# First chunk of each batch prepared ahead, last batch written out, and some loads and steps issued later

## The reference

```python
mod = (_silu(L0_c) @ L0_wmod).reshape(L0_c.shape[0], 6, 1, -1)
sa, ca, ga, sb, cb, gb = (mod[:, 0], mod[:, 1], mod[:, 2], mod[:, 3], mod[:, 4], mod[:, 5])
...
h = _layernorm(x, axis=-1) * (1 + ca) + sa
x = x + ga * _L0_attn_ref(h, L0_attn_Wqkv, L0_attn_bqkv, L0_attn_Wo, L0_attn_bo)
h = _layernorm(x, axis=-1) * (1 + cb) + sb
x = x + gb * _L0_ffn_ref(h, L0_ffn_gate_weight, L0_ffn_gate_up_proj, L0_ffn_down_proj, L0_ffn_old_to_new)
return x
```

## Time and profile before

| | |
|---|---|
| median of 3 runs | 4376.86 us (4376.18 to 4387.05) |
| profiled execution | 4383.56 us, of which the span of its instructions 4381.8 us |
| mean granted TensorE clock | 0.939 |
| busy share of the span | PE 88%, DVE 62%, POOL 63%, ACT 41% |
| first batch, from first to next first projection | 107.3 to 1053.2 us |
| experts, first to last PE work | from 3913.3 us |

### The profile page before, as it was taken

How to read it: one execution, slowest core, us unless ns; L and a number is a source line. 1 busy time by engine, 2 the same in 40 slices (tenths; PEclk the granted TensorE clock), 3 DMA queues, 4 the chain that set the end, 5 groups by cost and what they waited for, 6 DMA issues and landing times.

```text
span 4381.8 us, 85215 instructions
## 1 busy us (share of the span) xinstructions
PE 3863.3 (88%) x21344; PEld 2343.0 (53%) x21344; DVE 2732.0 (62%) x5837; ACT 1803.8 (41%) x3526; POOL 2773.6 (63%) x2251
## 2 busy tenths in 40 slices
PE   2989999886989998877899998869899998859998
PEld 1755544455744554456654454447555444547776
DVE  2767677455757766465667775457676774546555
ACT  1335555422345555333355554323355554211111
POOL 2768788723768878615678888407587886315454
PEclk7989999997989999988899999979899998979999
DMA  5443333243433334234433333324433332449998
GB/s 193 160 136 81 97 97 105 79 146 105 172 111 95 81 98 122 69 142 134 162 89 95 98 97 103 135 83 160 140 79 97 96 104 79 146 124 257 259 249 194
DMA packets 305622, 555.81 MB, mean 127 GB/s; under 512 B 59892, under 2 KB 99956, under 8 KB 301812
## 3 DMA queue, kind: packets, MB, share of 16 engines
q1 hardware_dynamic: 283640, 491.91, 37.6%
q0 software_dynamic: 21504, 58.40, 5.7%
HBM read 318.15 MB, written 174.85 MB: 113 GB/s over the span
## 4 chain that ended last, share of the span: by engine, by line
PE 60%; issue 14%; POOL 11%; DMA 6%; DVE 4%; ACT 2%; SPq 2%; DVEq 0%; POOLq 0%; ACTq 0%
PE PS L1293 16%; PE PS L1269 12%; PE PS L1246 12%; PE PS L1190 5%; PE PS L1390 4%; POOL qs L951 3%; POOL t L948 3%; PE PS L1401 2%; DMA out<-z,it 2%; POOL Sm L974 2%; DMA QK<-qkd 2%; POOL hTl L926 2%; PE PS L1327 2%; PE PS L1272 1%; SPq L681 1%
## 5 line engine op out<-in xcount | busy, mean ns | idle before, releaser
L1091 ACT ACTIVATE Pt<-PS 128x512 f32<-128x512 f32 (+3 forms) x2560 | 1204.3, 543 | 1069.7 <-PE PS L1269 613.0
L974 POOL TENSOR_TENSOR Sm<-Pt 128x512 f32<-128x512 f32 (+3 forms) x960 | 1028.3, 1077 | 451.7 <-ACT Pt L1091 448.9
L1570 DVE TENSOR_REDUCE part<-PS 128x1 f32<-128x512 f32 x1536 | 1003.7, 685 | 350.1 <-PE PS L1246 342.9
L1246 PE MATMUL PS<-QK 96*128 96x512 f32 (+3 forms) x2560 | 1033.6, 422 | 125.1 <-DMA QK<-qkd 51.1
L1269 PE MATMUL PS<-QK 97*128 97x512 f32 (+3 forms) x2560 | 996.7, 410 | 42.3 <-DMA QK<-mT 21.0
L1293 PE MATMUL PS<-Pt,V 128*32 128x512 f32 (+3 forms) x5120 | 873.5, 555 | 19.4 <-POOL Sm L974 19.3
L1297 PE MATMUL PS<-Sm,onesv 128*32 128x512 f32 (+3 forms) x1920 | 822.0, 536 | 0.0
L1566 DVE CUSTOM_DVE_ANT_0 PS<-PS,consts 128x128 f32<-128x128 f32 (+3 forms) x1024 | 504.0, 495 | 454.8 <-PE PS L1246 449.3
L1269 PEld LDWEIGHTS PS<-QK 97*128 97x128 f32 x2560 | 491.1, 194 | 477.8 <-issue 349.8
L974 POOL TENSOR_TENSOR Sm<-Sm,Pt 128x512 f32<-128x512 f32 (+1 forms) x640 | 712.2, 1113 | 50.2
L1246 PEld LDWEIGHTS PS<-QK 96*128 96x128 f32 x2560 | 501.5, 197 | 333.8 <-DVE part L1570 107.2
(11 more groups left out here) (164 smaller groups left out, 4821.9 us busy)
## 6 DMA issues: line engine op xcount, KB each, us to landing
QK<-qkd SPq DMA_DIRECT2D x720, 128.0 KB, 3.1
qkd<-st SPq DMA_DIRECT2D x64, 1024.0 KB, 4.5
Wg<-wgu SPq DMA_DIRECT2D x48, 768.0 KB, 5.6
o<-od SPq DMA_DIRECT2D x448, 64.0 KB, 2.0
W<-wd SPq DMA_DIRECT2D x4, 6144.0 KB, 21.6
Wd<-wdn SPq DMA_DIRECT2D x48, 384.0 KB, 7.2
xin<-x SPq DMA_DIRECT2D x16, 1024.0 KB, 7.6
vd<-vst SPq DMA_DIRECT2D x16, 1024.0 KB, 6.1
```

Of the source, the lines that this page charges most:

```text
L974: nc.gpsimd.tensor_tensor(total, of[0][:, first:CH] if i == 1 else total, of[i][:, first:CH], ALU.add).then_inc(sum_done, 1)
L1091: nc.scalar.activation(Pt[:, t % NPT, first:CH], S2[t % NS2][:, first:CH], ACT.Exp, scale=SCALE).then_inc(exp_done, 1)
L1246: mm(s1[:, 0:w], QK[0:3 * HD, hh % 2, 0, qb * P:(qb + 1) * P], QK[0:3 * HD, hh % 2, 1, c * CH:c * CH + w], start=True, stop=True).then_inc ...
L1570: v.reduce_max(part[:, qb, cc:cc + 1], s1[:, 0:w], AX.X).then_inc(s1_dve, 1)
```

## The change

Chunk 0 of a batch is no longer prepared by `front()`. For batch 0 its `stat`, `xhat`, turns, `upper` and `lower` stand in the setup, ahead of the loop; for batches 1 to 3 they stand in the third stage of the batch before, as the steps `lead_stat` (behind `old`, ahead of `new` of chunk 3), `lead_xhat` (behind `new`, ahead of `place`) and `lead` (ahead of the last `slot`). They use banks 0 and 1 of PSUM. The scales and shifts modb are copied in two halves. x and the rotary tables of the next batch are loaded behind W's reload; those of batch 0 near the start. SP's wait for the store of W is gone from the setup; ACT waits for it ahead of the first exponential. `batches` makes a loop of three passes and the fourth batch as code of its own behind it, with the number of the batch a constant; there the reload of W and the lead steps are left out. `load_attention` and `load_tokens` for j = 0 and 1 move from the end of hh = 14 into hh = 15, behind its stack, its row of maxima and `move(14, 0)`. The two `widen` steps go from rounds 211 and 217 to rounds 224 and 230. OUT_AT changes.

```diff
-    out = [("stat", 0), ("xhat", 0)]
-    for ct in range(KT):
-        out += parts(0, ct)
+    out = []
...
-OUT_AT = (8, 9, 10, 11, 12, 13, 14, 16)
+OUT_AT = (10, 10, 11, 12, 13, 14, 15, 16)
...
-    closing[NR * (H - 2) + 1].append(("widen", 0))
-    closing[NR * (H - 2) + 7].append(("widen", 1))
+    closing[last - 1].append(("widen", 0))
+    closing[last + 5].append(("widen", 1))
...
+        out += [("back", j, t) for t in range(TPC)] + [("old", j, 0), ("old", j, 1)]
+        if j == NCH - 1:
+            out.append(("lead_stat", j))
+        out.append(("new", j))
+        if j == NCH - 1:
+            out.append(("lead_xhat", j))
...
-    return out + [("slot", NCH - 1)]
+    return out + [("lead", NCH - 1), ("slot", NCH - 1)]
...
+        def batches(eng):
+
+            with eng.Fori(0, NB - 1) as b:
+                yield b
+            yield NB - 1
...
+            def load_lead(b):
+
+                sp.dma_start(xin[0][:, :, :], x[b, 0].rearrange("(t p) c -> p t c", p=P)).then_inc(x_in[0], 16)
+                load_tables(0)
+                load_tables(1)
+
+            load_lead(0)
             wait_apart(sp, mod_done, 1)
...
             sp.dma_start(wd, W[:, :, :, :, :].bitcast(F32)).then_inc(w_out, 16)
-            wait_apart(sp, w_out, 16)
...
-                load_input(0)
-                load_tables(0)
-                load_tables(1)
                 meet(sp, 2 * b + 1)
                 load_input(1)
...
                     move(hh - 1, 0)
+                    if hh == H - 1:
+                        for j in range(2):
+                            load_attention(j)
+                            load_tokens(j)
...
                     move(hh - 1, 2)
-                    if hh == H - 2:
-                        for j in range(2):
-                            load_attention(j)
-                            load_tokens(j)
...
-                sp.dma_start(W[:, :, :, :, :].bitcast(F32), wd).then_inc(w_in, 16)
+                if not last_batch(b):
+                    wait_apart(sp, w_out, 16)
+                    sp.dma_start(W[:, :, :, :, :].bitcast(F32), wd).then_inc(w_in, 16)
+                    load_lead(b + 1)
...
+            def power(b, j):
+
+                pool.wait_ge(var_ready, ONE + NCH * b + j + 1)
+                nc.gpsimd.tensor_tensor(rsA[:, :], rsA[:, :], K[:, K_MH:K_MH + TPC], ALU.pow).then_inc(rs_done, 1)
+
+            def lower(b, j, ct):
+
+                pool.wait_ge(h_upper, ONE + KT * (NCH * b + j) + ct + 1)
+                nc.gpsimd.tensor_tensor(hTl[:, j % 2, ct], hraw[:, j % 2, ct], hTu[:, j % 2, ct], ALU.subtract).then_inc(h_lower, 1)
+
+            power(0, 0)
+            for ct in range(KT):
+                lower(0, 0, ct)
+            for b in batches(pool):
...
+            def lead_parts(b):
+
+                act.wait_ge(modb_set, ONE + b + 1)
+                for ct in range(KT):
+                    act.wait_ge(turned, ONE + KT * NCH * b + ct + 1)
+                    nc.scalar.activation(hraw[:, 0, ct], PS[:, ct % 2], ACT.Identity,
+                                         bias=modb[:, ct:ct + 1], scale=modb[:, KT + ct:KT + ct + 1]).then_inc(led, 1)
+                    act.wait_ge(led, ONE + KT * b + ct + 1)
+                    nc.scalar.activation(hTu[:, 0, ct], hraw[:, 0, ct], ACT.Copy).then_inc(h_upper, 1)
...
+                    elif kind == "lead" and not last_batch(b):
+
+                        act.wait_ge(y_ps, ONE + TPC * NCH * (b + 1))
+                        lead_parts(b + 1)
...
+            def lead_turns(b):
+
+                pe.wait_ge(xhat_ready, ONE + TPC * (NCH * b + 1))
+                for ct in range(KT):
+                    if ct >= 2:
+                        pe.wait_ge(led, ONE + KT * b + ct - 1)
+                    for t in range(TPC):
+                        last = nc.tensor.transpose(PS[:, ct % 2, t * P:(t + 1) * P], xin[0][:, t, ct * P:(ct + 1) * P], ident)
+                    last.then_inc(turned, 1)
...
+            shifts(0)
+            spreads(0, 0)
+            normalised(0, 0)
+            for b in batches(dve):
                 meet(dve, 2 * b + 1)
-                v.tensor_copy(modb[:, :], modc[:, b, :]).then_inc(modb_set, 1)
+                v.tensor_copy(modb[:, 2 * KT:4 * KT], modc[:, b, 2 * KT:4 * KT])
...
+                    elif kind == "lead_stat":
+                        if not last_batch(b):
+                            shifts(b + 1)
+                            spreads(b + 1, 0)
+                    elif kind == "lead_xhat":
+                        if not last_batch(b):
+                            normalised(b + 1, 0)
```

More of the change, by code:

```diff
@@ L259, in routing @@
             out.append(("widen", 3))
-        out += [("back", j, t) for t in range(TPC)] + [("old", j, 0), ("old", j, 1), ("new", j)]
+        out += [("back", j, t) for t in range(TPC)] + [("old", j, 0), ("old", j, 1)]
[4 more added lines that the diff above has]
+            out.append(("lead_xhat", j))
         if more:
@@ L916, in _ @@
                     if kind == "stat":
[L918 to L920 removed]
+                        power(b, step[1])
                     elif kind == "lower":
[L923 to L926 removed]
+                        lower(b, *step[1:])
                     elif kind == "second":
@@ L986, in _ @@
                         widen(step[1])
+                    elif step[0] == "lead_stat" and not last_batch(b):
+                        power(b + 1, 0)
+                    elif step[0] == "lead" and not last_batch(b):
+                        for ct in range(KT):
+                            lower(b + 1, 0, ct)
                     elif step[0] == "join":
@@ L1027, in _ @@
             last.then_inc(w_upper, 1)
-            with act.Fori(0, NB) as b:
+            def lead_parts(b):
[6 more added lines that the diff above has]
+                    nc.scalar.activation(hTu[:, 0, ct], hraw[:, 0, ct], ACT.Copy).then_inc(h_upper, 1)
+            lead_parts(0)
+            for b in batches(act):
                 meet(act, 2 * b + 1)
@@ L1173, in _ @@
             last.then_inc(modT_ps, 1)
-            with pe.Fori(0, NB) as b:
+            def lead_turns(b):
+                pe.wait_ge(xhat_ready, ONE + TPC * (NCH * b + 1))
+                for ct in range(KT):
+                    if ct >= 2:
[3 more added lines that the diff above has]
+                    last.then_inc(turned, 1)
+            lead_turns(0)
+            for b in batches(pe):
                 meet(pe, 2 * b + 1)
@@ L1321, in _ @@
                         last.then_inc(u_ready, 1)
+                    elif kind == "lead":
+                        if not last_batch(b):
+                            pe.wait_ge(y_used, ONE + TPC * NCH * (b + 1))
+                            lead_turns(b + 1)
                     elif kind == "logit":
@@ L1463, in _, with spreads, normalised, shifts @@
             ck, cp = Chain(dve, chK, 8), Chain(dve, chP, 8)
-            with dve.Fori(0, NB) as b:
+            def spreads(b, j):
+                ci = NCH * b + j
+                a.begin(ci)
+                dve.wait_ge(x_in[j % 2], ONE + 32 * b + 16 * (j // 2) + 16)
+                for t in range(TPC):
+                    last = v.bn_stats(stA[:, t, :], xin[j % 2][:, t, :])
+                a.link(last, passed)
+                for t in range(TPC):
+                    last = v.bn_aggr(mvA[:, t, :], stA[:, t, :])
+                a.link(last)
+                v.tensor_scalar(rsA[:, :], mvA[:, :, 1], EPS, None, ALU.add).then_inc(var_ready, 1)
+                a.end()
+            def normalised(b, j):
+                own = xin[j % 2]
+                dve.wait_ge(rs_done, ONE + NCH * b + j + 1)
+                for t in range(TPC):
+                    v.tensor_scalar(own[:, t, :], own[:, t, :], mvA[:, t, 0:1], rsA[:, t:t + 1], ALU.subtract, ALU.mult).then_inc(xhat_ready, 1)
+            def shifts(b):
+                v.tensor_copy(modb[:, 0:2 * KT], modc[:, b, 0:2 * KT]).then_inc(modb_set, 1)
+            shifts(0)
+            spreads(0, 0)
+            normalised(0, 0)
+            for b in batches(dve):
                 meet(dve, 2 * b + 1)
-                v.tensor_copy(modb[:, :], modc[:, b, :]).then_inc(modb_set, 1)
+                v.tensor_copy(modb[:, 2 * KT:4 * KT], modc[:, b, 2 * KT:4 * KT])
                 def residual(j, t):
@@ L1509, in _ @@
                     if kind == "stat":
-                        j = step[1]
-                        ci = NCH * b + j
-                        own = xin[j % 2]
-                        a.begin(ci)
-                        dve.wait_ge(x_in[j % 2], ONE + 32 * b + 16 * (j // 2) + 16)
-                        for t in range(TPC):
-                            last = v.bn_stats(stA[:, t, :], own[:, t, :])
-                        a.link(last, passed)
-                        for t in range(TPC):
-                            last = v.bn_aggr(mvA[:, t, :], stA[:, t, :])
-                        a.link(last)
```

(11 more changed lines are left out.)

27 lines of the change are left out of this document (12 added, 15 removed).

## The result

The changed kernel takes 4264.51 us (median of 4 runs, 4260.46 to 4274.07), the kernel before in the same comparison 4381.95 us (4376.18 to 4389.52). The ratio is 0.9734, with a 95% interval of 0.9709 to 0.9759: faster, by 117 us. The forecast was 4276, from a gain of 100.6.

The account below looks back on a forecast made before the run. PE, busy 88% of the span, bounds the kernel; only its idle time can be won. 26.4 + 25.6 + 48.6 = 100.6 us off the profiled 4383.56 makes 4283.0, less 6.7 for the median: 4276.3; range 4240 to 4306.

Parts of the forecast that it names:

- Setup: Ahead of the first projection: SP's wait goes, 27.4 us gained, 1 charged for late bvg and x; bounds -27.4 and -25.
- Change of batch: Between batches: preparation leaves the path, 7.6 us gained at each of three changes, plus 2.8; bounds -41.2 and -22.8.
- `lower` under the tables: POOL's four subtractions beside DVE's bf16 operations take turns and delay Racc by 5.2 us; bounds 0 and 5.2.
- Heads 14 and 15: End of each batch: -12.85 (QK wait), -1.3 (widen), +2.0 (late POOL), -12.15 a batch, four times; bounds -72.2 and -19.
- My walk of POOL's list: Head 15: POOL's steps in order, scale(0) ending at 872.0, PE waiting 3.8 us for sums and losing 2.0.
- If POOL were on time, a gain of 3.9: Head 15: with POOL on time PE would end at 905.4 against 909.3, in place of a loss of 2.0.
- The fourth batch: Last change of batch: no jump back, DVE goes on 0.53 us behind the barrier against 3.54, saving 2.8 us.
- More: no turns: Rival: POOL and DVE don't hold each other up, POOL on time in head 15; 139.8 us gained, 4237; chance 0.20.
- the Aoh group unchanged under `lower`: Profile sign at the change of batch that would show POOL and DVE not holding each other up.
- The wait moves: Rival: head 15's maxima row and `move(14, 1)` wait behind the 3.5 MB; 30 us less gain, 4306; chance 0.14.
- Not what it says: Rival: `lead` not ready at the barrier or waited for behind it, changes of batch gain nothing; 4302; chance 0.07.
- Slower: Rival: fourth batch's straight-code instructions arrive late, 0.84 us for each of 120 packets deciding; 4390 or more; chance 0.03.

Follow-up runs that it names:

- bias_first: The changed kernel with bvg and x of chunk 1 loaded ahead of the store of W; 4265.21 us, ratio 0.9748.
- loads_back: The changed kernel with the attention and token loads for chunks 0 and 1 back at the end of hh = 14; 4321.94 us, ratio 0.9876.
- widen_small: The changed kernel with head 15's two widen steps made 1 column wide per tile in place of 512; 4234.87 us, ratio 0.9677.
- dve_widen: The changed kernel with head 15's two widen steps on DVE in place of POOL, in full; 4243.51 us, ratio 0.968.
- last_out_only: The kernel before with only the loop of three passes and the fourth batch as code of its own; 4372.17 us, ratio 0.9978.
- all_out: The changed kernel with all four batches written out as straight code, no loop over batches; 4248.77 us, ratio 0.9692.

## Why the prediction was right, step by step

- **Setup, -26.4.** The first projection came at 79.3 for 79.9: -28.0. The last part of the step, "of some 2 us I charge 1" for bvg and x behind the store of W, was too small: DVE waited 3.37 us for bvg, and the first row transpose of batch 0 stood 97.8 us behind the projection in place of 94.1. Net -24.3, just outside the bound of -25 (27.4 - 2 is 25.4). bias_first takes this wait away.
- **Change of batch, -25.6.** `lead_stat` was hidden, as said. `lead_xhat`: from gN to pos it is 3.02 us, 1.53 before: +1.5 for 1.6. The jump: 3.5 and 3.7 us from Racc to projection, 0.6 in the last, as worked out. What was mis-sized is `lower` under the tables, 5.2 us for what measured 3.95 less 0.9 that PE's slot won back (4.34 for 5.25 us, at a granted clock of 0.63 in place of 0.52). I let DVE stand for all of POOL's 5.25 us, and expected `lower` to take 10 us or more; it took 8.43. They do take turns, but both pay: DVE 3.95 us and POOL 3.2, and POOL's share is off the path. POOL's four took 1371, 2200 and up to 2775 ns each (shortest, median, longest), and the first came under Aoh, which still took 1.76 us: there POOL stood, as it had come second. So Racc came 4.5 to 4.7 us later, not 6.8, and the three changes gave 46.4 - 13.8 = 32.6 us. The Trainium skill ("SBUF — State Buffer", "SBUF: two separate sides") says that whichever of the two starts first has the port for its whole instruction and the other blocks; the traces agree (2.82 and 1.90 us of DVE beside POOL for 1.75 and 1.02 alone), and by it the cost is split by who comes first, which I should have walked through.
- **Heads 14 and 15, -48.6.** Without the wait for Q and K and the early widen I had 14.15 us a batch: the last step between rows fell by 14.2, 13.4, 14.3 and 17.6. loads_back shows that the queue was the cause. For the tail I had +2.0 from POOL being late, and it was +3.2, +2.9, +3.1 and -0.2. My walk of POOL's list held: taking off the 35.0 us by which head 15 starts earlier in batch 0, it had widen at 810.3 and 826.3 us, where they start at 810.18 and 827.52, and out at 837.3 for 839.07. I had one wait of PE, of 3.8 us; it was two, 1.64 and 2.39 us, 4.03 together. What the walk lacked is the lower clock around them: PE stood still for 1.5 us less than before the change and was still 3.2 us later, as its matmuls took 4.7 us more (rows under widen_small). Together -50.5. "If POOL were on time, a gain of 3.9" was too little: widen_small and dve_widen show 5.8 below the 65.2 of before. So the price that I put on POOL's lateness, 3.9 + 2.0 = 5.9 us, was 8.9, and that +2.0 came near +3.1 is in part luck: the two errors, of 1.9 and 3.0 us, work against each other.
- **The fourth batch, 2.8** in the step above, was right for the jump (0.6 us from Racc to the projection in place of 3.5 and 3.7), and wrong in that nothing else was asked of straight code: last_out_only measured 6 to 14 us. What of it lies beyond the jump and the 2.6 us by head 1 was not told from the scatter of single batches.
- **The rivals.** "More: no turns" falls with the longer B groups. The sign that I had named for it, the Aoh group unchanged under `lower`, did come (1.76 us), and would have misled: POOL came second there and stood itself. "The wait moves" didn't come: the loads are issued from 786.26 on, the maxima row behind them at 794.16, and PE waits for a maxima row only four times, once a batch at head 0 (5.5 us at most, 5.4 before). "Not what it says" would have shown a wait for hTl behind the barrier; there is none, PE is released by the barrier itself. "Slower" ends with all_out, which is straight throughout and faster; no late instructions show. The Trainium skill ("Runtime: NRT & Kernel Launch", "Instruction fetch mechanics") says that a taken branch can force a fetch; the runs agree in that DVE stands 3.54 us at a jump and 0.35 to 0.54 without, but that these 3 us are a fetch no run shows.

The terms, forecast and measured: setup 26.4 and 24.3, changes of batch 25.6 and 32.6, heads 48.6 and 50.5; the rest, 2.1 us, is scatter between batches, the inside of the straight batch, and the stage of the experts. The median came 12 us under the forecast: 9 by these terms, and 3 because the profiled execution of the changed kernel was the slowest of its four, 9.6 above their median, where that of before had been 6.7 above the median shown. The measured gain of 117 has 5 us more, because the kernel before took 4381.95 us in this comparison and 4376.86 when it was shown.

## What to carry to other kernels

When work moves under a DVE stretch, walk through both engines' lists instruction by instruction: two engines that take turns split the cost, and only the share of the one on the critical path counts. Before a load is issued early, ask which wanted transfer stands behind it on the same queue: 3.5 MB ahead of Q and K cost 12 to 13 us a batch, and a store of 6 MB ahead of a bias 3.4 of DVE and 2 to 4 of PE. A step that was moved to fit a transfer should then be given to the engine that has room there (9.1 us on POOL cost 8.9, the same work on DVE 1.6). And price a short wait of PE with the clock behind it: of those 8.9 us only 2.8 were PE standing still.

## What the runs showed of the hardware that I had not expected

- SP issues the same transfers faster in straight code than in a loop: twelve of Q and K in 6.90 us against 7.80. The addresses and the semaphore values are constants there; which of them it is was not tried.
- A short wait of PE can come with a low granted clock that costs more than the wait: in head 15, 2.8 us more of standing still came with 6.1 us more of matmul time. The 2.39 us of waiting that end at 835.92 are followed by 0.50 in 836 to 841. It doesn't follow from the length of the wait: the 1.56 us in batch 3 left the clock at 1.00 in 3588 to 3593, and the 5.17 us ahead of the first `out` in the kernel before were followed by 0.69 in 866 to 871 and then 1.00.
